# Block 1 attention: output of probabilities x values moved into a shared ring of four PSUM banks, opening matmuls of zeros taken out

## What is computed

```python
def _attn(xq, ctx, wq, wkv, wo, bo):
    q = _heads(xq @ wq)
    k, v = jnp.split(ctx @ wkv, 2, axis=-1)
    k = _heads(k); v = _heads(v)
    q = _rope(q, sq, cq); k = _rope(k, sk, ck)
    sim = jnp.einsum('bhnd,bhmd->bhnm', q, k) * DH ** (-0.5)
    a = jax.nn.softmax(sim, axis=-1)
    o = jnp.einsum('bhnm,bhmd->bhnd', a, v)
    o = o.transpose(0, 2, 1, 3).reshape(xq.shape[0], xq.shape[1], MID)
    return o @ wo + bo
x = _attn(attn_in, attn_in, sa_wq, sa_wkv, sa_wo, sa_bo) + x
x = _attn(cross_in, ctx_n, ca_wq, ca_wkv, ca_wo, ca_bo) + x
```

## Time and profile before

| | us |
|---|---|
| median of 3 runs | 4405.24 |
| profiled execution, its own time | 4406.8 |
| its span in the trace | 4404.7 |
| TensorE matmul busy (PE) | 4152.3 |
| VectorE busy (DVE) | 2959.4 |
| ScalarE busy (ACT) | 2745.7 |
| GpSimd busy (POOL) | 2758.7 |
| TensorE on the chain that ended last | 65% |
| granted TensorE clock, mean | 0.985 |

### The profile page before, as it was taken

One profiled execution on the slowest core, in us unless ns is written; L12 is line 12 of the kernel. 1 busy time (PEld: TensorE's weight loads), 2 busy tenths in 40 slices (PEclk: granted clock), 3 DMA queues, 4 the chain that ended last, 5 costly groups with the idle time before them and its releaser, 6 DMA issues.

```text
span 4404.7 us, 95930 instructions
## 1 busy us (share of the span) xinstructions
PE 4152.3 (94%) x34934; PEld 3522.3 (80%) x34934; DVE 2959.4 (67%) x6250; ACT 2745.7 (62%) x10788; POOL 2758.7 (63%) x2555
## 2 busy tenths in 40 slices
PE   6999998888889999999999999999999999999999
PEld 5777777777779987888888888778787878788998
DVE  6999999888865555655555555666666666665443
ACT  4889988888863335666566656665656565655333
POOL 3666666666667775555555555566666666665776
PEclk8999999999999999999999999999999999999999
DMA  2000011111111122222222222322222222221111
GB/s 69 30 30 30 31 42 45 44 38 37 49 50 44 49 74 75 73 75 73 75 73 73 74 74 88 104 73 87 73 87 73 87 73 87 73 93 61 49 45 33
DMA packets 228997, 276.65 MB, mean 63 GB/s; under 512 B 37932, under 2 KB 160304, under 8 KB 228528
## 3 DMA queue, kind: packets, MB, share of 16 engines
q1 hardware_dynamic: 228528, 270.53, 18.0%
HBM read 85.89 MB, written 50.33 MB: 31 GB/s over the span
## 4 chain that ended last, share of the span: by engine, by line
PE 65%; DVE 19%; ACT 8%; issue 5%; POOL 2%; DMA 0%; SPq 0%; ACTq 0%; POOLq 0%; DVEq 0%
PE BANKS L569 15%; PE BANKS L571 14%; PE BANKS L570 14%; PE BANKS L720 6%; PE BANKS L708 6%; PE BANKS L756 5%; DVE NM L983 4%; DVE PT L990 3%; ACT PR L869 2%; ACT PR L853 2%; DVE WL L1032 1%; DVE Z L1089 1%; ACT HF L897 1%; PE BANKS L764 1%; DVE ST L1079 1%
## 5 line engine op out<-in xcount | busy, mean ns | idle before, releaser
L1168 POOL TENSOR_TENSOR PR<-PR,RL 128x512 f32<-128x512 f32 x1024 | 1069.3, 1045 | 948.5 <-DVE RL L995 945.2
L869 ACT ACTIVATE PR<-BANKS,NM 128x128 f32<-128x128 f32 x2048 | 729.9, 384 | 488.0 <-DVE NM L1046 431.1
L853 ACT ACTIVATE PR<-BANKS,NM 128x128 f32<-128x128 f32 x2048 | 728.3, 413 | 3.5 <-DVE NM L983 3.4
L569 PE MATMUL BANKS<-HH,WH 128*128 128x512 f32 x1632 | 692.4, 424 | 35.6 <-DVE SN L1060 25.7
L1046 DVE TENSOR_REDUCE NM<-BANKS 128x8 f32<-128x1024 f32 x256 | 312.6, 1221 | 532.7 <-PE BANKS L720 532.6
L756 PE MATMUL BANKS<-ID,PR 128*128 128x128 f32 x4096 | 633.0, 278 | 39.8 <-DVE OL L1039 23.8
L571 PE MATMUL BANKS<-HH,WL 128*128 128x512 f32 x1632 | 644.4, 395 | 0.0
L570 PE MATMUL BANKS<-HL,WH 128*128 128x512 f32 x1632 | 644.3, 395 | 0.0
L756 PEld LDWEIGHTS BANKS<-ID,PR 128*128 128x128 f32 x4096 | 496.2, 142 | 163.1 <-issue 62.5
L853 ACT ACTIVATION_READ_ACCUMULATOR PR<-BANKS,NM 128x1 f32 x2048 | 517.2, 254 | 0.0
L1191 POOL TENSOR_TENSOR GL<-GF,GH 128x512 fp32r<-128x512 f32 x256 | 342.6, 1338 | 206.0 <-DVE GH L1135 206.0
(11 more groups left out here) (123 smaller groups left out, 10881.2 us busy)
## 6 DMA issues: line engine op xcount, KB each, us to landing
SW<-SN SPq DMA_DIRECT2D x1024, 128.0 KB, 2.0
x_scratch<-X SPq DMA_DIRECT2D x80, 512.0 KB, 3.2
X<-x_scratch SPq DMA_DIRECT2D x80, 512.0 KB, 4.0
CX<-in_ctx SPq DMA_DIRECT2D x32, 384.0 KB, 4.2
X<-in_x SPq DMA_DIRECT2D x16, 512.0 KB, 3.8
out<-X SPq DMA_DIRECT2D x16, 512.0 KB, 2.9
CX<-in_ctx SPq DMA_DIRECT2D x32, 128.0 KB, 4.1
STG<-in_L_xcond_W SPq DMA_DIRECT2D x4, 512.0 KB, 5.0
```

What stands on the lines that cost most here:

```text
L569: e.matmul(o, lh, rh, start=first and i == 0, stop=False)
L853: made = e.activation(pr[:, r], bank[:, r], ACT.Exp, bias=nm[:, h:h + 1], accum_out=RL[npr(t)[0]][:, h:h + 1])
L869: made = e.activation(pr[:, r], bank[:, r], ACT.Exp, bias=nm[:, h:h + 1], accum_out=RL[npr(t)[0]][:, h:h + 1])
L1168: e.tensor_tensor(p3, p3, RL[npr(t)[0]][:, :].unsqueeze(2).broadcast_to([128, 4, 128]), ALU.mult).then_inc(s_nrm, 1)
```

## The change

It does two things. First, pv no longer has bank 5 to itself: the ring of three becomes RING1 = (0, 1, 4, 5), and pv, v1, q1, k1, the probability transposes and the turns of block 1's attention all go round it. Since Banks gives each use the bank of the use four before it, and pv is now one of them, the waits ahead of each stage change. Second, the two matmuls of zeros per group are gone, with ZR, its memset and its semaphore; the first real matmul into each output bank of a group has start=True instead.

```diff
-            ZR = sb("ZR", [128, 128], R, stack=second)
...
-        UP, TWO, THREE, FOUR = (0, 1), (4, 5), (0, 1, 4), (4, 5, 6, 7)
+        UP, TWO, RING1, FOUR = (0, 1), (4, 5), (0, 1, 4, 5), (4, 5, 6, 7)
...
-                tp.add(("o", x.i), (5,), s_ol, o_use(x) + 1)
+                tp.add(("o", x.i), RING1, s_ol, o_use(x) + 1)
...
-                tp.add(("v1", p, g, m), THREE, s_va, v_use(p, g, m) + 1)
+                tp.add(("v1", p, g, m), RING1, s_va, v_use(p, g, m) + 1)
...
-                tp.add(("q1", x.i), THREE, s_rt, 2 * x.i + 1)
+                tp.add(("q1", x.i), RING1, s_rt, 2 * x.i + 1)
...
-                tp.add(("k1", x.i), THREE, s_rt, 2 * x.i + 2)
+                tp.add(("k1", x.i), RING1, s_rt, 2 * x.i + 2)
...
-                tp.add(("p", t.n), FOUR if t.n < NL0 else THREE, *pt_done(t))
+                tp.add(("p", t.n), FOUR if t.n < NL0 else RING1, *pt_done(t))
...
-                    tp.add((stage, x), FOUR if x.p < 2 else THREE if KIND[x.p] == "b" else TWO, s_hf, len(hparts))
+                    tp.add((stage, x), FOUR if x.p < 2 else RING1 if KIND[x.p] == "b" else TWO, s_hf, len(hparts))
...
                     if x.j == 0:
-                        q.wait_ge(s_zr, 1)
                         for i in range(2):
                             q.wait_ge(*tp.free(("y", x.p, x.g, i)))
-                            e.matmul(PS[6 + i][:, :].rearrange("p (r t) -> p r t", r=4), ZR[:, :], ZR[:, :].unsqueeze(1).broadcast_to([128, 4, 128]),
-                                     start=True, stop=False)
...
-                                     [(OH1[k][:, b, :], OL1[k][:, b, :], wh[:, x.j, :], wl[:, x.j, :])], False, x.j == 7 and b % 2 == 1)
+                                     [(OH1[k][:, b, :], OL1[k][:, b, :], wh[:, x.j, :], wl[:, x.j, :])], x.j == 0 and b % 2 == 0, x.j == 7 and b % 2 == 1)
```

More of the change, by code:

```diff
@@ L331, in build @@
         s_oh, s_ol, s_y = sem("oh"), sem("ol"), sem("y")
-        s_qk, s_rt, s_zz, s_v1, s_va, s_zr = (sem(k) for k in ("qk", "rt", "zz", "v1", "va", "zr"))
+        s_qk, s_rt, s_zz, s_v1, s_va = (sem(k) for k in ("qk", "rt", "zz", "v1", "va"))
         s_sw = [sem(f"sw{i}") for i in range(2)]
@@ L707, in _ @@
                             h = 64 * (2 * (x.j % 4) + e_)
-                            made = e.matmul(PS[5][64 * e_:64 * e_ + 64, 128 * b:128 * b + 128], V1[4 * (x.j // 4) + b][:, h:h + 64],
+                            made = e.matmul(PS[tp.bank(("o", x.i))][64 * e_:64 * e_ + 64, 128 * b:128 * b + 128], V1[4 * (x.j // 4) + b][:, h:h + 64],
                                             PT[(2 * x.i + e_) % NPT1][:, 128 * b:128 * b + 128], start=True, stop=True)
@@ L858, in _ @@
                     q.wait_ge(s_y, o_use(x) - 1)
-                    e.activation(OH1[x.i % 2][:, :, :], PS[5][:, :].rearrange("p (c t) -> p c t", c=4), ACT.Copy).then_inc(s_oh, 1)
+                    e.activation(OH1[x.i % 2][:, :, :], PS[tp.bank(("o", x.i))][:, :].rearrange("p (c t) -> p c t", c=4), ACT.Copy).then_inc(s_oh, 1)
                 for t in at["exp", tick]:
@@ L1063, in _ @@
                     q.wait_ge(s_oh, o_use(x) + 1)
-                    e.tensor_tensor(OL1[x.i % 2][:, :, :], PS[5][:, :].rearrange("p (c t) -> p c t", c=4), OH1[x.i % 2][:, :, :].bitcast(F),
+                    e.tensor_tensor(OL1[x.i % 2][:, :, :], PS[tp.bank(("o", x.i))][:, :].rearrange("p (c t) -> p c t", c=4), OH1[x.i % 2][:, :, :].bitcast(F),
                                     ALU.subtract).then_inc(s_ol, 1)
@@ L1160, in _ @@
             for tick in ticks:
-                if tick == T0[3] - 14:
-                    q.wait_ge(s_y, NL0 // 4)
-                    e.memset(ZR[:, :].bitcast(F), 0.0).then_inc(s_zr, 1)
                 for t in at["normal", tick]:
```

## The result

The changed kernel takes 4483.2 us in the median of 4 runs (4474.8 to 4487.9), against 4408.5 us for the kernel before measured beside it. The ratio is 1.0163 with a 95% interval of 1.0149 to 1.0176: about 72 us slower. The profiled execution has a span of 4477.2 us, 72.5 us more than the 4404.7 of before. The forecast was 4490 us, slower. It started from a median of before of 4405.2 us and added 85; against 4408.5 the same sum would have given 4494, so 3 of the 11 us by which the sum was off don't show in the time, by chance.

What follows compares the result with a forecast made beforehand. TensorE's own stream was taken to bound passes 3 and 4 (busy 1150 of 1166 and 1107 of 1164 us). Terms +129.8 - 16.0 - 28.7 = +85.1 us on a 4405.2 us median gave 4490 us, range 4455 to 4535.

Steps and rivals of the forecast that it cites:

- The mechanism: TensorE's q1 in 219 units waits for VectorE's OL, behind KT and SN, instead of SN; with v1 and context turns +129.8 us.
- q1 in pass 3: Plain units of pass 3: q1's second matmul 0.42 us later from waiting for OL, in 112 units, +47.0 us.
- q1 in pass 4: q1 already waits for SN in pass 4; the distance from SN to OL, 0.60 us, added in 107 units, +64.2 us.
- v1 and context turns: At groups' turns, 15 v1 of pass 3 and 16 first context turns wait for OL instead of SN, 0.60 us each, +18.6.
- The zeros: Two matmuls of zeros per group removed ahead of out: 0.50 us saved in each of 32 groups, -16.0 us.
- The turns: Odd-tick and second context turns no longer wait for v1's copy: -4.5 us in pass 3, -14.1 and -10.1 in pass 4.
- Weight loads: q1's load starts only after the release; were it pulled ahead, pass 3 would lose some 12 us less (112 x 0.12).
- The relief: Rival, chance 0.13: the turns' relief doesn't arrive in pass 4 because ScalarE holds TensorE; 24.2 us gone, 4514 us.
- pv waited no more often: Rival, chance 0.09: pv or another further use becomes late near turns, one unit in four losing 0.6 us; 38 us, 4528.
- the order of instructions: Rival, chance 0.03: q1's bank isn't pv's in most units, so no wait comes; 0 to -45 us left.
- The signs: Expected: OL releasing q1 220 to 250 times, units 0.42 and 0.60 longer, TensorE about 94% and 91% busy, other passes unchanged.
- rival 2: Chance 0.05: the wait ahead of q1 is absorbed by shorter waits behind it, making the kernel faster; at zero loss 4360 us.

Runs made afterwards that it cites:

- e8: e4 with one wait instead of two: q1 that waited for SN and OL of the same even tick waits for OL alone; 4496.7 us, ratio 1.0196.
- e3: Changed kernel with VectorE writing OL ahead of the rotary form of k1, after the maximum of the scores; 4321.1 us, ratio 0.9803.
- e1: Kernel before with only the 64 matmuls of zeros and their tile taken out, banks as before; 4394.6 us, ratio 0.9963.
- e2: Kernel before with only pv put into the shared ring of four banks, zeros kept; 4495.6 us, ratio 1.0198.
- e7: Kernel before, zeros kept, with only the odd tick's turn and context turn moved to bank 5, pv's bank; 4375.5 us, ratio 0.9911.
- e5: e1 with VectorE's OL moved ahead of the rotary form of k1, banks as before; 4427.4 us, ratio 1.0032.
- e4: Kernel before, banks and zeros untouched, with an added wait for OL ahead of the 219 q1 that have it in the changed kernel; 4511.9 us, ratio 1.0232.

## Why the prediction was right, point by point

**The mechanism** was the one forecast, and it is shown from both sides: the wait alone costs 94 us (e8), and with OL early the changed kernel's banks, zeros out as there, take 86 us less than the kernel before (e3). The sum of +85.1 us came out as +74.0 in the framed time. The term that was off most is q1 in pass 4. Term by term:

**q1 in pass 3 (+47.0).** The step was 0.42 us a unit. From one unit's OL to the next it was 2412.59 - 2403.85 = 8.74 us before, by the earlier trace rows and the following unit's row,

```profile
2412.59 0.68 DVE L1064 TENSOR_TENSOR OL<-BANKS,OH 128x512 fp32r<-128x512 f32 x1
```

and it is 2430.65 - 2421.47 = 9.18 after, so 0.44.

```profile
2430.65 0.68 DVE L1060 TENSOR_TENSOR OL<-BANKS,OH 128x512 fp32r<-128x512 f32 x1
```

This is right, also in taking the second matmul rather than the first load as the mark (0.53 would have given 59 us).

**q1 in pass 4 (+64.2).** The step of 0.60 us was right for a plain unit (read in the same way, 8.35 before and 8.95 after), but the count of 107 was not. Fifteen of them belong to the unit ahead of a group's turns, in which VectorE also has the norms of the next group. Before, q1 stood for 1.30 us there already. These are TensorE's rows of that place before (q1, then the next two pv):

```profile
3168.09 0.50 PE L569 MATMUL BANKS<-HH,WH 128*128 128x512 f32 x1 [1.30 <-DVE SN L1060]
...
3173.32 1.09 PE L708 MATMUL BANKS<-PT,V 128*64 128x128 f32 x16
...
3184.79 1.09 PE L708 MATMUL BANKS<-PT,V 128*64 128x128 f32 x16
```

And after (q1, transposes, turn, pv; context turn, transposes, second context turn, pv):

```profile
3222.92 0.50 PE L568 MATMUL BANKS<-HH,WH 128*128 128x512 f32 x1 [1.30 <-DVE OL L1060]
...
3224.41 0.60 PE L755 MATMUL BANKS<-ID,PR 128*128 128x128 f32 x4
3224.84 0.60 PE L763 MATMUL BANKS<-ID,Z 128*128 128x128 f32 x4
...
3226.78 1.09 PE L707 MATMUL BANKS<-PT,V 128*64 128x128 f32 x16
...
3232.39 0.63 PE L774 MATMUL BANKS<-ID,CX 128*128 128x128 f32 x4 [1.20 <-DVE OL L1060]
...
3235.42 0.60 PE L755 MATMUL BANKS<-ID,PR 128*128 128x128 f32 x4
3235.85 0.60 PE L774 MATMUL BANKS<-ID,CX 128*128 128x128 f32 x4
...
3237.78 1.09 PE L707 MATMUL BANKS<-PT,V 128*64 128x128 f32 x16
```

q1 waits for 1.30 us in both kernels, once for SN and once for OL. Between the q1 before and this one VectorE had no pause in which to be later or earlier:

```profile
3158.00:3168.10 10.10, 8.80 (x71) 7.02 (x69) 9.89 (x28) 4.98 (x21) 6.54 (x6) 1.00 0.14 52
```

It was busy for 9.89 of 10.10 us. OL to OL is then as long as SN to SN, and the switch costs nothing: 15 x 0.60 = 9 us of the term didn't arise. The rows of this late unit were in the trace of before; I multiplied a plain unit's price by all units. No run takes the late units by themselves; this is read from the rows.

**v1 and context turns (+18.6).** The context turn waits 1.20 us for OL in the rows above, where it was 0.60 for SN: the 0.60 counted. No run has these waits alone.

**The zeros (-16.0).** 13.6 us in e1, 15.6 between e2 and the changed kernel. Right within 2.4 us. The Trainium skill's figure in "TensorE: Matmul & The Clock Gate", section "Back-to-back issue gap", would have given 8.4 us, and e1 speaks against it here.

**The turns (-28.7).** In pass 4 the turn now starts 3224.84 - 3224.41 = 0.43 us behind the transposes and the second context turn 0.43 too, as the unhindered one did. e7 gives -24.7 us for the three together, 4 us less than counted; why stays open. In the changed kernel more came back in the stretch with the context turns than I had counted: pv to pv took 11.47 us before and 11.00 after, 0.47 less, where +0.60 for the wait and -0.63 for the second turn leave 0.03. The other 0.44 us, 7 us in all, are the small waits of v1 and q1 there on copies of the same ticks, which I had seen and left out of the sum (they were the reason for its end of 38).

Together: in pass 4, 41.6 - 9 - 7 leaves 26, against 27.2 measured; in pass 3, 43.5 and 2 for the step of 0.44 give 46, against 46.8. This doesn't mean that each part is right by itself: added up from the runs it is +94.3 (e8), -13.6 (e1) and -24.7 (e7), with +18.6 as counted for v1 and the context turns, 74.6 in all. That sum agrees partly by chance, since e8 already holds a relief of the turn that e7 counts again, and the 7 us above are in none of these runs.

**Weight loads.** In every row shown here where q1 really waited, its weight load started 0.05 to 0.11 us behind the release, so it isn't pulled ahead of its own wait. The prediction called this a disagreement with the Trainium skill, and that was too much: the table at the head of "TensorE: Matmul & The Clock Gate" has weight loads pulled ahead of matmuls in flight, and says nothing of a load that itself carries a wait. The price that the prediction gave for it, 112 x 0.12, is 13.4 us and not some 12.

**The rivals.** The relief did arrive (e7), the wait wasn't absorbed except in the late units, pv waited no more often than before, and the order of instructions did bring the wait.

**The signs.** The step of a plain unit, the waits of the turns, the missing row and the other passes came out as listed (pv starts at 1700.5 us after 1702.0, and 378.5 us follow the last start in both). The busy shares fell less than forecast, and OL ended 205 waits of weight loads, not 220 to 250. One sign of being wrong did come: the fifteen late units have the wait ahead of q1 and are no longer for it. That is rival 2 in one unit of a group of pass 4, at a price of 9 us.

## What to carry to other kernels

Before a buffer is put into a shared ring, write down for each use which reader releases the slot it will get, and where that reader stands in its engine's own order: here the ring was good and the reader two instructions too late, and moving that one instruction turned 72 us lost into 87 us won. Such a pair of edits has to be judged together, since each was a loss by itself (+90 us for the ring in e2, +33 us for the order in e5) and both together won 73 us (e3 against e1). And a price per unit should be multiplied only by the units in which the waiting engine, not the one it waits for, sets the pace: a delay ahead of a unit that waits anyway, for SN or for a copy, is partly taken back there.

## What the runs showed of the hardware that I had not expected

A weight load with waits for two semaphores ahead of it started 0.11 us behind the release, one with a single semaphore 0.05 to 0.06 us behind it (e4 and e8, the same program otherwise). The trace shows where it goes: the second wait is an instruction of its own on TensorE's queue, which takes 51 ns (EVENT_SEMAPHORE). From 1700 to 4150 us e4 has 1051 of them there and e8 862. Over the 219 uses this is worth 7 us in the framed time and 15 us between the medians of the two (4511.9 and 4496.7), whose intervals lie just apart (from 1.0217, and up to 1.0214).

Instructions of VectorE that are recorded with 0.68 us each follow each other at 0.60 us (the rows of OL, KT and SN in e3), and one that was put between others cost 0.39 (e5): neither duration nor spacing alone gives the price.
